# Attention's output projection with W_O as the weights and z as the 512 moving columns

## What is computed

```python
x = x + 0.5 * ffn(layernorm(x))
q, k, v = (einsum('ahe,bce->bach', W, layernorm(x)) for W in (W_Q, W_K, W_V))   # 16 heads of 64
attn = softmax(where(causal, k q^T, -1e10) / 8)
z = einsum('bacC,baCh->bach', attn, v)
x = x + einsum('aeh,bach->bce', W_O, z)
x = x + 0.5 * ffn(layernorm(x))
# ffn: router logits, the best 2 of 8 experts, softmax over these two,
#      sum of weight * (relu(x W1 + b1) W2 + b2), hidden width 512
```

## Time and profile before

| | |
|---|---|
| runs of the kernel | 1006.35, 1007.69, 1008.24 us, median 1007.69 |
| span of the profiled execution, first to last instruction | 1005.9 us |
| attention's steps | from 208 us to 833 us of the span |
| TensorE busy in the whole span | 948.2 us, 94% |
| weight loads (beside the products) | 807.2 us, 80% |
| VectorE, ScalarE, GpSimd | 825.8, 711.5, 287.7 us |

### The profile page before, as it was taken

How to read it: one execution, slowest core, us unless ns; L and a number is a source line. 1 busy time by engine, 2 the same in 40 slices (tenths; PEclk the granted TensorE clock), 3 DMA queues, 4 the chain that set the end, 5 groups by cost and what they waited for, 6 DMA issues and landing times.

```text
span 1005.9 us, 24244 instructions
## 1 busy us (share of the span) xinstructions
PE 948.2 (94%) x7677; PEld 807.2 (80%) x7677; DVE 825.8 (82%) x3091; ACT 711.5 (71%) x1954; POOL 287.7 (29%) x316
## 2 busy tenths in 40 slices
PE   3689899989999999999999999999999998999993
PEld 3579899968777777878787878787878777899993
DVE  7878787768789789879888979878978987997785
ACT  3457677667777878777878777878777777577771
POOL 3777100251111111312221312120200213467654
PEclk9769999999999999999999999999999999999997
DMA  9348655412121113112112112111111123457685
GB/s 250 107 132 259 182 163 158 124 54 45 25 44 33 34 30 47 40 44 39 45 39 45 36 48 38 45 40 34 40 39 26 43 54 113 134 158 219 168 252 163
DMA packets 90622, 90.22 MB, mean 90 GB/s; under 512 B 30080, under 2 KB 66848, under 8 KB 90496
## 3 DMA queue, kind: packets, MB, share of 16 engines
q1 hardware_dynamic: 77296, 67.79, 24.9%
q0 software_dynamic: 8640, 18.76, 7.4%
q10 hardware_dynamic: 4560, 2.12, 0.8%
HBM read 63.95 MB, written 24.67 MB: 88 GB/s over the span
## 4 chain that ended last, share of the span: by engine, by line
PE 80%; DVE 9%; DMA 3%; ACT 3%; issue 2%; SPq 1%; POOL 1%; DVEq 0%; POOLq 0%; ACTq 0%
PE psum L1813 14%; PE psum L1802 13%; PE psum L1759 12%; PE psum L1663 10%; PE psum L1632 7%; PE psum L1633 7%; PE psum L1634 7%; PE psum L1821 6%; PE psum L1641 2%; ACT arena L804 1%; PE psum L1584 1%; DVE arena L1365 1%; DMA xg<-x_slots 1%; DVE bn L909 1%; PE psum L1577 1%
## 5 line engine op out<-in xcount | busy, mean ns | idle before, releaser
L804 ACT ACTIVATE arena<-arena,neg_max 128x512 f32<-128x512 f32 (+3 forms) x512 | 281.2, 556 | 1.6 <-DVE neg_max L1365 1.6
L1365 DVE CUSTOM_DVE_ANT_0 arena<-psum,causal 128x512 f32<-128x512 f32 (+3 forms) x512 | 217.3, 483 | 3.0 <-PE psum L1759 3.0
L812 ACT ACTIVATE arena<-psum 128x512 f32<-128x512 f32 x192 | 107.8, 596 | 141.8 <-PE psum L1802 141.8
L1813 PE MATMUL psum<-arena 128*64 128x512 f32 (+3 forms) x1024 | 152.0, 439 | 0.7 <-DVE arena L1378 0.7
L762 ACT ACTIVATE arena<-psum,b_t 128x256 f32<-128x256 f32 x312 | 122.5, 474 | 42.1 <-PE psum L1634 41.9
L1663 PE MATMUL psum<-w_sb,arena 128*128 x1248 | 151.9, 275 | 0.0
L1802 PE MATMUL psum<-ident,arena 128*128 128x128 f32 x1280 | 150.5, 273 | 1.1 <-ACT arena L804 0.6
L606 POOL DMA_INDIRECT arena<-y_tiles,y_at x64 | 61.0, 953 | 302.8 <-PE psum L1759 197.9
L1663 PEld LDWEIGHTS psum<-w_sb,arena 128*128 128x128 f32 x1248 | 146.2, 192 | 0.0
L1802 PEld LDWEIGHTS psum<-ident,arena 128*128 128x128 f32 x1280 | 141.9, 141 | 1.7 <-ACT arena L804 0.7
L1813 PEld LDWEIGHTS psum<-arena 128*64 128x64 f32 x1024 | 68.0, 136 | 83.9 <-issue 74.0
(11 more groups left out here) (216 smaller groups left out, 1960.7 us busy)
## 6 DMA issues: line engine op xcount, KB each, us to landing
w_raw<-in_L_ffn_W_dram SPq DMA_DIRECT2D x78, 256.0 KB
arena<-inv_dram SPq DMA_DIRECT2D x128, 128.0 KB, 3.1
xg<-x_slots SPq DMA_DIRECT2D x78, 144.0 KB
y_tiles<-y_sb SPq DMA_DIRECT2D x39, 128.0 KB, 2.0
arena<-y_rows SPq DMA_DIRECT2D x16, 256.0 KB, 4.3
x_slots<-blank SPq DMA_DIRECT2D x18, 144.0 KB
out_dram<-xs ACTq DMA_DIRECT2D x8, 256.0 KB, 2.5
y_rows<-y_sb,y_tok POOLq DMA_INDIRECT x78, 3.1
```

What stands on the lines that cost most here:

```text
L804: ins = act.activation(prob_tile(i, h, t), prob_tile(i, h, t), ACT.Exp, scale=-1.0, bias=neg_max[i % 2][:, h, t:t + 1], accum_out=row_sum[ ...
L812: act.activation(four_turned(g), turned_bank(i, g), ACT.Copy).then_inc(pt_act, 1)
L1365: ins = dve.tensor_tensor_reduce(out=prob_tile(i, h, t), in0=score_tile(t, h), in1=causal[:, SEQ - (t + 1) * P:SEQ], scale=-1.0, scalar=-2 ...
L1813: ins = pe.matmul(RING_C[m, k * P:SEQ], v_sb[i // V_PAIRS % 2][:, k, col:col + DH], probs_t[:, h * 10 * P + PT_COL[k]:h * 10 * P + PT_COL[ ...
```

## The change

For the batches 0 to 6 project_out loads wo_t of the pair as weights and lets z_sb flow as 512 columns, one fp32 product in place of four. The bank then holds the sum turned: outputs on the partitions, tokens in the columns. In step s = 1 of the next batch ScalarE copies the bank to the new tile o_turned (take_out), TensorE turns its four squares into RING_A (turn_out), and VectorE adds RING_A to xs (add_out), now behind the subtractions for k and q. The next batch's first projection waits for the copy (o_taken), no longer for the addition. Batch 7 keeps the four products and the addition from O_BANK. norms(b) is put in the chain behind add_out.

```diff
@@ -169,6 +169,7 @@
 inv_sum = [sb(f"inv_sum{i}", [P, 2, QT]) for i in range(2)]
+o_turned = sb("o_turned", [P, SEQ])
 inv_dram = nc.dram_tensor("inv_dram", [2, 2, P, QT], fp32).ap()
@@ -340,6 +341,8 @@
 o_ps = sem("o_ps")
+o_taken = sem("o_taken")
+o_back_ps = sem("o_back_ps")
 o_added = sem("o_added")
@@ -427,6 +430,7 @@
 TURN_STEP, PUT_STEP, JOIN_STEP = 4, 4, 5
+BACK_STEP = 1
 KEY_STEP, ORDER_STEP, LIST_STEP = 2, 3, 5
@@ -805,6 +809,10 @@
+    def take_out(b):
+        act.wait_ge(o_ps, PAIRS * (b + 1))
+        act.activation(o_turned[:, :], O_BANK, ACT.Copy).then_inc(o_taken, 1)
+
     def transposed(i):
@@ -830,6 +838,8 @@
             exps(i, 1, [2])
+            if b > 0 and s == BACK_STEP:
+                take_out(b - 1)
             if s == TURN_STEP and b + 1 < BATCH:
@@ -1388,8 +1398,11 @@
     def add_out(b):
-        dve.wait_ge(o_ps, PAIRS * (b + 1))
-        dve.tensor_tensor(batch_of(b), O_BANK.rearrange("p (t d) -> p t d", t=QT), batch_of(b), ALU.add).then_inc(o_added, 1)
+        if b + 1 < BATCH:
+            dve.wait_ge(o_back_ps, b + 1)
+        else:
+            dve.wait_ge(o_ps, PAIRS * (b + 1))
+        dve.tensor_tensor(batch_of(b), (RING_A if b + 1 < BATCH else O_BANK).rearrange("p (t d) -> p t d", t=QT), batch_of(b), ALU.add).then_inc(o_added, 1)
         dve.wait_ge(o_added, b + 1)
@@ -1457,13 +1470,12 @@
             if s == 1:
-                if b > 0:
-                    add_out(b - 1)
-                else:
+                if b == 0:
                     work = next_measures(0)
                 if b == BATCH - 1:
                     work = chain_of(work, seek_tiles(1, 0, next_row[1]))
-                work = chain_of(work, norms(b))
+                if b == 0:
+                    work = chain_of(work, norms(b))
             if i == STEPS - 2:
@@ -1492,6 +1504,9 @@
                 work = place_rows(U1 + BATCH - 2, RING_A)
+            if b > 0 and s == BACK_STEP:
+                add_out(b - 1)
+                work = chain_of(work, norms(b))
             go_on(work, 5)
@@ -1759,9 +1774,17 @@
+    def turn_out(b):
+        pe.wait_ge(o_taken, b + 1)
+        for t in range(QT):
+            ins = pe.transpose(RING_A[:, t * P:(t + 1) * P], o_turned[:, t * P:(t + 1) * P], ident[:, :])
+        ins.then_inc(o_back_ps, 1)
+
     def ring_a_taken(i):
         b, s = divmod(i, PAIRS)
+        if b > 0 and s == BACK_STEP:
+            pe.wait_ge(o_added, b)
         if s == TURN_STEP and b + 1 < BATCH:
@@ -1816,7 +1839,11 @@
         pe.wait_ge(z_ready, i + 1)
-        wait(pe, o_added, i // PAIRS)
+        if i // PAIRS < BATCH - 1:
+            wait(pe, o_taken, i // PAIRS)
+            pe.matmul(O_BANK, wo_t[:, pair_cols(i)], z_sb, start=(i % PAIRS == 0), stop=(i % PAIRS == PAIRS - 1)).then_inc(o_ps, 1)
+            return
+        wait(pe, o_taken, BATCH - 1)
         for t in range(QT):
@@ -1855,6 +1882,8 @@
                 transpose_x(1, 0)
+            if b > 0 and s == BACK_STEP:
+                turn_out(b - 1)
             if s == TURN_STEP and b + 1 < BATCH:
                 turn_for_attention(b + 1)
             if b > 0 and s == route_step(b):
```

## The result

The changed kernel takes 1029.62 us (median of four, 1028.42 to 1032.21) against 1007.8 for the kernel before (four runs, 1006.35 to 1008.24): ratio 1.022, 95% interval 1.0205 to 1.0235. The profiled execution is the slowest of the four, 1032.21 us, with a span of 1030.2 us, 24.3 above that of before.

What follows compares the result with a forecast made beforehand. TensorE, busy for 94% of the span and without holes in attention's steps, was taken as the bound. Hole and squares +21.6, projection -1.7, waits for z -0.3 gave +19.6 on 1007.7: 1027.3 us, range 1022 to 1035.

Steps and rivals of the forecast that it cites:

- The wait: Second step of seven batches: TensorE idles 2.4 us before the turned squares, until ScalarE's queued bank copy is done.
- The squares: Second step of seven batches: four turned squares take 0.63 us up to attend, including 0.10 for an uncovered first load.
- Hole and squares: Second step of seven batches: attend starts 3.08 us later, +21.6 us over seven.
- The projection: Steps of the first seven batches: each new product group takes 0.96 us, 0.03 less than before, -1.7 us over 56.
- the cheap record (rival 1): Projection: a full-width 512-column record is one pass, group 0.56 us, total -2.7 us, 1005.0 us; chance 0.06.
- start 0.43 apart: Projection, sign of being right: the new product's two records start 0.43 us apart and the group takes 0.96.
- What hides: Second steps and after: ScalarE's 0.60 us delay, VectorE's later addition (0.4 us to spare) and later norms cost nothing.
- waits for z: Attention: three us of rest let VectorE catch up, so some of TensorE's 0.5 us of these waits go, -0.3 us.
- The clock: Attention: granted clock stays at 1.00 throughout, since TensorE once idled 1.93 us and kept it; chance of falls 0.10.
- rival 3: Second steps: ScalarE's copy is there when TensorE comes, only squares are paid, +1.3 us, 1009.0 us; chance 0.03.
- rival 2: Second steps: clock falls in the 2.4 us rest, 2.2 us lost each time, +15 over seven, 1042.7 us; chance 0.10.
- the forecast mechanism: Attention: TensorE's wait and squares outweigh the shorter projection, +19.6 us in all; chance 0.81.

Runs made afterwards that it cites:

- e2: Changed kernel without the four turned squares, TensorE still waiting for ScalarE's copy, sum added turned: 1021.44 us, ratio 1.0136.
- e1: Changed kernel with ScalarE's bank copy moved ahead of its three copies of turned squares in the second step: 1008.58 us, ratio 1.001.
- e3: Kernel before with only the projection changed for seven batches, no copy or squares, sum added turned: 1005.94 us, ratio 0.9977.
- e4: Changed kernel with the old projection's four products of 128 columns in all batches, copy, squares and addition kept: 1035.43 us, ratio 1.0278.
- d1: Changed kernel with ScalarE's bank copy directly behind the copy of q, ahead of both exponentials: 1018.83 us, ratio 1.0111.
- s1: Changed kernel with the bank copy directly behind the copy of q and the four squares turned four times over: 1028.15 us, ratio 1.0197.
- d2: Changed kernel with ScalarE's bank copy between the two exponentials: 1022.67 us, ratio 1.0156.
- p1: Changed kernel with the four turned squares moved behind attend in TensorE's order, ScalarE's copy left in place: 1017.63 us, ratio 1.009.
- s3: Changed kernel with ScalarE's bank copy early (no hole) and the four squares turned eight times over: 1030.26 us, ratio 1.0216.

## Why the prediction was right, and where not

- *The wait.* Forecast: hole 2.4 us, copy of the bank in the place of the copy of v. Measured 2.36, seven times, and alone in e2, away in e1. This is the term that decided, and it was right.
- *The squares.* Forecast 0.63 from the first to attend behind a wait, measured 0.59 (637.48 to 638.07); 0.44 a step where the copy is there in time (e1).
- *Hole and squares.* Forecast 3.08 a step, measured 3.02: 21.1 us and not 21.6.
- *The projection.* Forecast 0.03 a group, measured 0.03 (0.995 to 0.963), 1.8 us. A record of 512 columns takes 0.43, about twice the 0.23 of a one-pass fp32r product; the cheap record (rival 1) is out. The sign "start 0.43 apart" left out the first load, which the sum has: the second record starts 0.53 behind the first, the next group 0.43 behind the second. The Trainium skill, "FP8 and Floating Point Precision", TensorE Precision Notes, gives a true fp32 product four passes through the array. The trace agrees: 2 x 0.43 us is near four times 0.213.
- *What hides.* ScalarE's delay, VectorE's addition (done at 640.10, wanted from attend's end at 640.44) and the later norms cost nothing, as forecast: the other steps are as long as in e3, but for the third one that a fall reaches. Of the waits for z 0.2 us is gone and not 0.3, and not for the reason given, the rest of three us: it is gone in e1 and e3 as well, which have no such rest.
- *The clock.* This term was wrong. The forecast had 1.00 throughout attention and gave the fall a chance of 0.10. It fell in three of seven, 5.0 us, and once in the stage before, 1.6 us. The step that failed is "it has idled 1.93 and kept it; 2.4 lies between": one execution of one hole was taken for a safe bound. The hole at that place is 1.6 to 2.2 us long in the other runs; a fall follows in the changed kernel's and in seven of the twelve experiments'. The upper bound was none either: the row of 990.90 to 994.60 in the earlier trace rows ends just ahead of a fall, as the next stretch shows.

```profile
994.70:1005.00 10.30, 0.00 (x0) 0.00 (x0) 4.69 (x8) 0.00 (x0) 0.25 (x1) 0.50 0.69 190
```

A clock still at 1.00 inside a hole says nothing yet: in attention the falls began from 1.3 us before to 1.5 us behind the hole's end. The price, 2.2 us a fall by the low stretch at 62, was 1.4 to 1.7 here. That stretch is the end of one that began at 39.0, so that its 4.4 us are not the length of a fall.
- *The covered wait* (rival 3) is what e1 makes true: 1009.0 forecast for it, 1008.58 measured.

The result lies in the range for the forecast mechanism plus a part of rival 2, for which the range left room. That the median is only 2.3 us above the forecast of 1027.3 is partly luck. Without its four falls the profiled span would be 1030.2 - 5.0 - 1.6 = 1023.6, 1.9 below the 1025.5 forecast, so that errors of both signs meet. How many falls the three runs without a profile had is not recorded. The forecast's own range is also a little wider than its terms give: 56 times -0.01 to +0.03 and 7 times 0.2 come to 1025.3 to 1030.4, not 1024.5 to 1031.

That no fall followed seven holes of 2.36 us in e2, where the changed kernel and e4 had three each, stays open; each is one profiled execution. The seven holes of e2 come 81.85 us apart, each time to 0.01, so that one situation may have repeated itself seven times; they are hardly seven separate trials. The holes of d1 and s1, and nearly those of d2, are as evenly spaced.

## What to carry to other kernels

When one engine paces a stage without holes, ask of each instruction added to it what releases it, and read in the releaser's own list what stands ahead: here two exponentials and a copy that needed the pacing engine's last product. Put the feeding instruction where its engine already waits (e1: 21 us for two moved lines). A product with fewer weight loads gained here only what its loads had left uncovered: one of eight was, and it is still there.

## What was not expected of the hardware

The granted clock falls behind some short holes and not behind others, more often the longer they are. In profiled executions, in attention, it fell behind 0 of 28 holes of at most 1.8 us (d1, d2, s1 and the third steps' 0.8 to 0.9 us in p1), 6 of 21 of 2.36, 8 of 14 of 2.85 and 7 of 7 of 3.82. Each of the 21 falls put the clock at 0.50, in all but two for 3.4 us (6.8 in those), and cost 1.4 to 1.7 us in the second and third steps together where it was that long. Turned squares kept it at 1.00, 32 in a row (s3).

In the stage ahead the length does not decide alone: the hole near 112 us was followed by no fall where it lasted 2.05 us (s1) and by one where it lasted 1.85 (e4). Behind a hole of 1.94 in the last stage of s3 the clock fell too. So a hole of 1.85 us is not safe, and what else decides is not shown. One fall more or less moves an execution by some 1.5 us, part of the 3.5 by which 23 runs of the kernel before differ (1006.0 to 1009.5).
